# A selective-scan and gated-expert kernel: opening reordered, and one row tile of each batch transposed a phase later

## The reference, cut to what matters

```python
# B=4 batches, L=512 steps, 512 channels, 16 states, 512 model columns
x_in  = in_proj_w @ ctx                       # 512 channels x 512 steps, batch by batch
u     = silu(causal_conv4(x_in) + conv_b)
dt_lo, Bm, Cm = split(x_proj_w @ u)           # 16 + 16 + 16 rows: the small projection
delta = softplus(dt_proj_w @ dt_lo + dt_proj_b)
for t: state = state * exp(delta_t * A) + (delta_t * u_t) * B_t     # per channel, 16 states
       y_t   = sum_n state[n] * C_t[n]
y     = (y + D * u) * silu(layernorm(x))
x2    = x + tanh(g_xattn) * y
h     = layernorm(x2)
sc    = h @ Wr.T; g = softmax(sc) kept at its top 2 and normalised
out   = x2 + tanh(g_ffn) * sum_s g_s (h @ U_s) @ V_s * (0.9 + 0.2 * g @ aw)
```

## Time and profile before

| | us |
|---|---|
| median of 3 runs | 594.83 (594.62 to 600.63) |
| the profiled execution | 593.71 |
| its span in the trace | 592.0 |
| PE busy | 516.1 (87%) |
| POOL busy | 483.2 (82%) |
| DVE busy | 458.4 (77%) |
| ACT busy | 395.5 (67%) |

### The profile page before, as it was taken

How to read it: one execution, slowest core, us unless ns; L and a number is a source line. 1 busy time by engine, 2 the same in 40 slices (tenths; PEclk the granted TensorE clock), 3 DMA queues, 4 the chain that set the end, 5 groups by cost and what they waited for, 6 DMA issues and landing times.

```text
span 592.0 us, 9391 instructions
## 1 busy us (share of the span) xinstructions
PE 516.1 (87%) x3162; PEld 392.7 (66%) x3162; DVE 458.4 (77%) x839; ACT 395.5 (67%) x702; POOL 483.2 (82%) x362
## 2 busy tenths in 40 slices
PE   6658689898985999999969999999699998999686
PEld 2147579767875697769668787677566765676453
DVE  3648799978976999779887999786677878788630
ACT  2366476958773878487946787578579777987321
POOL 0088779979998999979997999699889998888700
PEclk9768899999977999999988999999999999999969
DMA  4198000006520001045220000075000000000000
GB/s 88 40 335 304 2 0 2 37 6 219 172 72 0 2 1 54 0 148 197 90 72 2 19 2 18 6 262 184 19 19 0 19 18 19 19 3 18 19 1 35
DMA packets 17986, 37.29 MB, mean 63 GB/s; under 512 B 5505, under 2 KB 6017, under 8 KB 17938
## 3 DMA queue, kind: packets, MB, share of 16 engines
q1 hardware_dynamic: 17938, 36.69, 17.9%
HBM read 32.23 MB, written 4.46 MB: 62 GB/s over the span
## 4 chain that ended last, share of the span: by engine, by line
PE 52%; POOL 22%; ACT 10%; issue 8%; DVE 5%; DMA 1%; DVEq 0%; POOLq 0%; ACTq 0%; SPq 0%
PE p_s L676 15%; POOL state L504 12%; PE p_y L695 11%; POOL dbu L491 6%; PE p_v L727 5%; PE p_f L718 4%; PE p_tr L644 4%; DVE state L1110 3%; PE p_pr L608 3%; ACT da L895 2%; POOL pair_b L467 2%; PE p_pr L601 1%; PE p_s L601 1%; PE p_pr L619 1%; ACT L847 1%
## 5 line engine op out<-in xcount | busy, mean ns | idle before, releaser
L504 POOL TENSOR_TENSOR state<-state,c_bc 128x1024 f32<-128x1024 f32 (+1 forms) x160 | 307.4, 1929 | 39.4 <-DVE state L1110 36.5
L1110 DVE TENSOR_TENSOR_SCAN state<-da,p_s 128x512 f32<-128x512 f32 (+1 forms) x160 | 175.7, 1105 | 58.3 <-PE p_s L676 54.6
L676 PEld LDWEIGHTS p_s<-pair_b,du_t 128*128 128x128 f32 x1280 | 171.4, 202 | 38.2 <-issue 23.0
L676 PE MATMUL p_s<-pair_b,du_t 128*128 128x128 f32 x1280 | 185.5, 288 | 6.8 <-ACT du_t L853 5.3
L695 PE MATMUL p_y<-ident,state 128*128 128x128 f32 x1024 | 151.7, 277 | 0.5 <-POOL state L504 0.5
L895 ACT ACTIVATE da<-delta,a_neg 128x512 f32<-128x512 f32 (+1 forms) x192 | 120.2, 642 | 25.1 <-DVE state L1110 24.8
L695 PEld LDWEIGHTS p_y<-ident,state 128*128 128x128 f32 x1024 | 121.7, 143 | 20.8 <-issue 18.3
L491 POOL TENSOR_TENSOR dbu<-du,pair_b 128x1024 f32<-128x1024 f32 (+1 forms) x64 | 116.5, 1820 | 0.1
L1110 DVE TENSOR_TENSOR_SCAN state<-p_s,dbu 128x512 f32<-128x512 f32 (+1 forms) x96 | 98.6, 1032 | 1.9 <-POOL dbu L491 1.9
L895 ACT ACTIVATE p_s<-delta,a_neg 128x512 f32<-128x512 f32 (+1 forms) x128 | 73.4, 579 | 38.4 <-DVE state L1110 37.8
L718 PE MATMUL p_f<-u_sb,h_t 128*128 128x512 f32 x112 | 55.2, 595 | 1.5 <-DVE gw L1197 1.5
(11 more groups left out here) (170 smaller groups left out, 624.8 us busy)
## 6 DMA issues: line engine op xcount, KB each, us to landing
c_bc<-bc_rows SPq DMA_DIRECT2D x32, 512.0 KB, 5.9
pair_b<-bc_rows SPq DMA_DIRECT2D x12, 512.0 KB, 5.5
xs<-in_x SPq DMA_DIRECT2D x16, 256.0 KB, 7.4
out<-ot SPq DMA_DIRECT2D x14, 256.0 KB, 2.0
cx<-in_ctx_t SPq DMA_DIRECT2D x4, 512.0 KB, 3.6
u_sb<-in_u_w SPq DMA_DIRECT2D x1, 1024.0 KB, 13.6
v_sb<-in_v_w SPq DMA_DIRECT2D x1, 1024.0 KB, 15.6
out<-state SPq DMA_DIRECT2D x2, 256.0 KB, 2.0
```

The lines of the kernel that those rows point to most:

```text
L504: eng.tensor_tensor(pair, pair, c_bc[:, 2 * p:2 * p + 2, c0:c0 + w], ALU.mult).then_inc(po_cs, 1)
L676: mm = eng.matmul(p_s[g % BANKS][:, t * P:(t + 1) * P], du_t[:, f % 2, t, :], diagonals_of(n // 2)[:, n % 2, c0 // P + t, :], start=(t == ...
L1110: eng.tensor_tensor_scan(slot(g)[:, 0:w], decayed, added, first, ALU.mult, ALU.add).then_inc(ve_scan, 1)
```

## The change

Opening: the small projection takes each block when its u is there, and `in_projection(4)` with its conv moves behind it. x of batches 0 and 1 and the weights U are loaded ahead of the store of B and C instead of among and behind the broadcasts. The z statistics and `scale_of_z(0)` move ahead of phase 0. For states 0 and 1 of phase 0 DVE makes du and dt\*u\*B itself (`first_dbu`), from a broadcast of B's pair 0 that is new; POOL's `times_u(0)` falls away and its diagonals of pair 0 are made after `times_c(0, 0)`. The exponential for A and the two tanh of the gates move ahead of the small projection's copy. From phase 1 on: for T = 0, 4, 8, 12 `normed` moves from n = 15 to n = 0 of the next phase, `turn_h` to its n = 1, `copy_h` from n = 1 to n = 2, and in phases with k = 0 `scale_of_f` stands ahead of `times_c(f, 5)`.

```diff
@@ which tiles have their dt*u*B made where
+    def on_dve(f, n):
+        return f == 0 and n < 2
-    PE_TILES = [(f, n) for f in range(F) for n in range(NS) if not on_pool(f, n)]
+    PE_TILES = [(f, n) for f in range(F) for n in range(NS) if not on_pool(f, n) and not on_dve(f, n)]
-    DIAGONALS = [(b, p) for b in range(B) for p in pe_pairs(b) if not by_act(b, p)]
+    DIAGONALS = [(0, p) for p in pe_pairs(0)[1:] + [0]]
+    DIAGONALS += [(b, p) for b in range(1, B) for p in pe_pairs(b) if not by_act(b, p)]
...
+        def wait_for_du(eng, f):
+            if f:
+                eng.wait_ge(po_du, f)
+            else:
+                eng.wait_ge(ve_du, 1)
@@ SP
+            for k in range(Q):
+                load_x(0, k)
             eng.wait_ge(pe_in, Q)
             load_ctx(1)
-            store_bc(0)
-            broadcast_b(0, 2)
-            broadcast_c(0, 0)
-            broadcast_c(0, 1)
-            broadcast_b(0, 5)
-            for p in range(2, 5):
-                broadcast_c(0, p)
-            for k in range(Q):
-                load_x(0, k)
-            for p in range(5, PAIRS):
-                broadcast_c(0, p)
             for k in range(Q):
                 load_x(1, k)
             eng.dma_start(u_sb[:, :, :], u_w.rearrange("(c p) n -> p c n", p=P)).then_inc(s_uv, 16)
+            store_bc(0)
+            broadcast_b(0, 0)
+            broadcast_c(0, 0)
+            broadcast_b(0, 2)
+            broadcast_c(0, 1)
+            broadcast_c(0, 2)
+            broadcast_b(0, 5)
+            for p in range(3, PAIRS):
+                broadcast_c(0, p)
             eng.dma_start(v_sb[:, :, :], v_w.rearrange("(c p) n -> p c n", p=P)).then_inc(s_uv, 16)
@@ POOL, diagonals, times_u, times_b
+                if (b, p) == (0, 0):
+                    eng.wait_ge(ve_dbu, 2)
...
+                if f == 1:
+                    eng.wait_ge(ve_dbu, 2)
...
+                elif i == 1:
+                    eng.wait_ge(ve_scan, 2)
                 if p == pool_pairs(b)[0]:
-                    eng.wait_ge(po_du, f + 1)
+                    wait_for_du(eng, f)
@@ POOL, order of work
-            diagonals(0, 0)
+            scale_of_z(0)
             diagonals(0, 1)
-            times_u(0)
+            diagonals(0, 2)
             times_b(0, pool_pairs(0)[0])
-            for i in range(2, len(pe_pairs(0))):
+            for i in range(3, len(pe_pairs(0))):
                 diagonals(0, i)
             for f in range(F):
...
                 times_c(f, 0)
+                if f == 0:
+                    diagonals(0, 0)
...
                 if turning:
                     diagonals(b + 1, 0)
+                if k == 0 and STATS.get(f):
+                    scale_of_f(STATS[f][0])
                 times_c(f, 5)
...
-                if STATS.get(f):
+                if k and STATS.get(f):
                     scale_of_f(STATS[f][0])
...
-                if f == 0:
-                    scale_of_z(0)
                 times_c(f, 6)
@@ PE
             def small_projection(b, blocks):
-                eng.wait_ge(ve_u, Q * b + Q)
                 for k in blocks:
+                    eng.wait_ge(ve_u, Q * b + Q if b else k + 1)
...
             def dt_projection(f):
...
                 if f:
                     eng.wait_ge(ve_dl, f)
+                if f > 1:
                     eng.wait_ge(ve_u, min(f + Q, BLOCKS))
...
             eng.wait_ge(s_first, 16)
-            for q in range(5):
+            for q in range(Q):
                 in_projection(q)
             eng.wait_ge(s_second, 16 * 6)
             eng.wait_ge(po_k, 9)
             small_projection(0, range(Q))
             dt_projection(0)
             turn_b(0)
+            in_projection(4)
             turn_du(0)
...
+                    if n == 1 and mid >= 0 and mid % Q == 0:
+                        turn_h(mid)
                     if n == 2:
...
-                    if n == 15 and Q <= f < EARLY + Q:
+                    if n == 15 and Q <= f < EARLY + Q and f % Q:
                         turn_h(f - Q)
@@ ACT
             tanh_v(Q - 1)
-            conv_first(4)
+            eng.wait_ge(s_second, 16 * 6)
+            eng.activation(a_neg[:, :, :], a_neg[:, :, :], ACT.Exp).then_inc(ac_k, 1)
+            eng.wait_ge(s_w, 16 * 5)
+            eng.activation(gx[:, :], gx[:, :], ACT.Tanh).then_inc(ac_k, 1)
+            eng.activation(gf[:, :], gf[:, :], ACT.Tanh).then_inc(ac_k, 1)
...
-            copy_du(0)
...
                     if f == 0 and n == 1:
+                        copy_du(0)
+                        conv_first(4)
+                    if f == 0 and n == 5:
                         tanh_v(4)
...
-                    if n == 1 and mid >= 0:
+                    if n == 0 and mid >= 0 and mid % Q == 0:
+                        normed(mid)
+                    if n == (1 if mid % Q else 2) and mid >= 0:
                         copy_h(mid)
...
-                        if Q <= f < EARLY + Q:
+                        if Q <= f < EARLY + Q and f % Q:
                             normed(f - Q)
@@ DVE
             def scan(f, n):
...
-                if on_pool(f, n):
+                if on_dve(f, n):
+                    eng.wait_ge(ve_dbu, n + 1)
+                    decayed, added = p_s[g % BANKS][:, :], dbu[:, 1, n, :]
+                elif on_pool(f, n):
...
+            def first_dbu(n):
+                if n == 0:
+                    eng.wait_ge(s_bbc[0], 16)
+                eng.tensor_tensor(dbu[:, 1, n, :], du[:, :], rows_of_b(0)[:, n, :], ALU.mult).then_inc(ve_dbu, 1)
...
-            taps(4)
...
+            for q in range(Q):
+                z_statistics(q)
             combine(0)
+            eng.wait_ge(ve_dl, 1)
+            eng.tensor_tensor(du[:, :], delta[:, 0, :], u[:, 0, :], ALU.mult).then_inc(ve_du, 1)
+            eng.wait_ge(ve_du, 1)
+            first_dbu(0)
+            first_dbu(1)
...
                     scan(f, n)
-                    if f == 0 and 8 <= n < 8 + Q:
-                        z_statistics(n - 8)
-                    if f == 0 and n == 4:
+                    if f == 0 and 2 <= n < 5:
+                        tap(4, n - 1)
+                    if f == 0 and n == 6:
                         silu_u(4)
```

More of the change, by code:

```diff
@@ L251, in flamingo @@
         ve_zs = sem("dve_z_statistics")
+        ve_du = sem("dve_du")
+        ve_dbu = sem("dve_dbu")
         ve_scan = sem("dve_scanned")
@@ L328, in broadcasts_of_b @@
         def broadcasts_of_b(b, p):
-            return sum(p in pool_pairs(a) for a in range(b + 1))
+            return sum(p in pool_pairs(a) for a in range(b + 1)) + (p == 0)
         ZOPS = 6
@@ L457, in diagonals @@
                     return
-                if i == 0:
+                if (b, p) == (0, 0):
+                    eng.wait_ge(ve_dbu, 2)
+                if i == 0 or b == 0:
                     eng.wait_ge(ac_turn, TURN["b", b] + 1)
@@ L474, in times_u @@
                 eng.wait_ge(ve_dl, f + 1)
-                if f:
-                    eng.wait_ge(pe_turn, TURN["du", f - 1] + 1)
-                    eng.wait_ge(po_dbu, by_pool[f, pool_pairs(b)[0]])
+                eng.wait_ge(pe_turn, TURN["du", f - 1] + 1)
+                eng.wait_ge(po_dbu, by_pool[f, pool_pairs(b)[0]])
+                if f == 1:
+                    eng.wait_ge(ve_dbu, 2)
                 eng.tensor_tensor(du[:, 0:w], delta[:, f % 2, 0:w], u[:, (Q * b + k) % U_RING, c0:c0 + w],
@@ L665, in make_dbu @@
                 g = NS * f + n
-                if n == 0:
+                if n == 0 or g == 2:
                     eng.wait_ge(ac_turn, TURN["du", f] + 1)
-                if by_act(b, n // 2):
+                if b == 0 and n == 0:
+                    eng.wait_ge(po_diag, DIAGONALS.index((0, 0)) + 1)
+                elif by_act(b, n // 2):
                     if k == 0 and c0 == 0:
@@ L748, in _ @@
                 for n in range(NS):
-                    if not on_pool(f, n):
+                    if (f, n) in by_pe:
                         make_dbu(f, n)
@@ L885, in decay @@
                     eng.wait_ge(ve_dl, f + 1)
-                if on_pool(f, n):
+                if (f, n) not in by_pe:
                     if g >= BANKS:
@@ L979, in _ @@
             copy_b(0)
-            eng.wait_ge(s_second, 16 * 6)
-            eng.activation(a_neg[:, :, :], a_neg[:, :, :], ACT.Exp).then_inc(ac_k, 1)
             softplus(0, 2)
-            copy_du(0)
             eng.wait_ge(ve_k, 4)
@@ L994, in _ @@
                     if f == 0 and n == 1:
+                        copy_du(0)
+                        conv_first(4)
+                    if f == 0 and n == 5:
                         tanh_v(4)
-                    if f == 0 and n == 3:
-                        eng.wait_ge(s_w, 16 * 5)
-                        eng.activation(gx[:, :], gx[:, :], ACT.Tanh).then_inc(ac_k, 1)
-                        eng.activation(gf[:, :], gf[:, :], ACT.Tanh).then_inc(ac_k, 1)
+                    if f == 0 and n == 4:
```

(6 more changed lines are left out.)

## The result

| | before | changed |
|---|---|---|
| median, us | 595.12 (594.62 to 600.63) | 564.53 (564.01 to 565.71) |
| ratio, 95% interval | | 0.947 (0.941 to 0.953) |
| span of the profiled execution | 592.0 | 562.3 |
| first scan | 38.40 | 31.88 |
| opening and phases 0 to 3 | 152.3 | 138.4 |

The median fell by 30.6 us, where 26.3 were forecast. A phase is counted from its first scan to the next phase's. All phases that aren't in the table (7, 10, 11, 14, 15, 18, 19) agree within 0.1 us. So the places are the two that the prediction names: the opening with phases 0 to 3 brings 13.9, the four ends 5.3 + 6.5 + 4.3 + 0.5 = 16.6, and the close behind the last scan takes 0.8 longer: 29.7 in the profiled executions. The other 0.9 of the 30.6 is how the two profiled executions lie to their medians.

The account below looks back on a forecast made before the run. Bounds by phase: POOL and DVE in 2, PE and POOL in 6, PE in 9; POOL for the opening's gain. 11.5 + 4.6 + 5.6 + 3.8 + 0.8 = 26.3 off 593.7 gives 567.4, plus 1.1: 568.5 us; range 560 to 579.

Parts of the forecast that it names:

- Small projection: Opening: last two blocks priced at the slow clock, 3.6 us, ending at 24.5, 2.4 earlier; 4.2 earlier at full clock.
- First scan at 32 to 34: Sign for the opening: scan 0 starts at about 32.8 instead of 38.40 us.
- z's scale before 29: Sign for the opening: `scale_of_z` comes before 29 us, its work lying in POOL's and DVE's idle time.
- POOL bounds: 11.5: Opening and first batch: POOL's chain limits the gain to 11.5 us, between 9 and 14.
- the DVE count: First batch by DVE's work alone: phase 1 at 60.4, phase 2 at 84.4, 14 us earlier than 98.35.
- the 85 to 88: Sign for the first batch: phase 2 begins at 85 to 88 us.
- The ends: Ends of phases 4, 8, 12, 16: moving h removes PE's waits, gaining 4.6, 5.6, 3.8 and 0.8 us.
- the rival that POOL takes it: Ends: only what POOL follows at once is gained, 6.4 instead of 14.8 us, giving 577; chance 0.2.
- One sign: Ends of phases 4, 8, 12: PE waits no more than 1 us for h.
- Only changes place: Ends: POOL's scale merely swaps places with one `times_c` of 2.34 us.
- The clock's return: Phases 9 and 13 back at full clock: 28.5 instead of 31.0 us, and 1.58 us from 20.23 to 18.65.
- The port rule: Opening: DVE instructions with two SBUF inputs and POOL's exclude each other; du could wait 1.09, DVE's 14 becoming 12.9.

Follow-up runs that it names:

- the repetition: The changed kernel run once more with no edit, on another chip beside two later edits: 565.05 us, ratio 0.953.
- the two with filling for PE: Changed kernel with extra identity transpositions in PE's opening waits: 563.77 us; the same plus POOL's broadcast wait filled with diagonals: 566.39 us.
- filled-POOL kernel: Changed kernel with three more POOL diagonals ahead of its first product and B's pair 2 broadcast ahead of C's pair 0: 566.55 us.
- h-only kernel: Kernel before with only the four h moved, including POOL's scale ahead of `times_c(f, 5)`: 580.42 us, ratio 0.974.
- opening-only kernel: Changed kernel with `normed`, `turn_h`, `copy_h` and `scale_of_f` put back in their old places: 585.28 us, ratio 0.982.

## Why the prediction was right, and where its sum was short

**Small projection: both prices are real.** I took the slow one, 3.6, and an end at 24.5. The profiled execution shows 1.93 and an end at 22.8; the same code in the repetition shows 3.45. Of the eight profiled kernels with the small projection block by block and no filling for PE, two show 1.93 and six 3.43 to 3.68; the two with filling for PE show 1.93. Whether TensorE has its higher clock at 20 us differs from one execution to the next. The end comes 1.1 earlier with the fast one, but the first scan only 0.3 (31.9 and 32.2): in the first execution DVE's du and products met POOL's diagonals (0.93 and 2.06), in the second they came after them (0.69 and 1.29). From the projection's end to delta's it was 6.1 us in both, where I had carried over 6.2; delta was there at 28.9 and 30.0, forecast 30.7.

**First scan at 32 to 34:** 31.9, forecast 32.8. In part luck: delta came 1.8 earlier than forecast, and DVE's du and products took 3.0 instead of 2.1. The broadcast was early enough. The first one went out at 25.25 (forecast 26.9), and the first three landed 3.5, 5.4 and 7.6 us after issue, for 3.8 to 8.5 of the first four in the earlier trace rows.

**z's scale before 29:** 27.95. Right, but its worth was hidden in a count of the whole phase. Putting it back made phase 4 start 11.4 us later.

**"POOL bounds: 11.5". This step failed.** POOL's forecast of its first `times_c` of phase 1 (66.3) was nearly met, at 65. But the rule drawn from it, that the batch gains only what POOL gains, was wrong. The phases' starts moved as I had worked out for DVE alone: phase 1 at 60.5 (60.4), phase 2 at 84.5 (84.4, a gain of 13.9), and phase 4 came 13.9 earlier. That the DVE count fits so closely is luck in part: the first scan was 0.9 earlier than in it and phase 0 1.1 longer (28.7, not 27.6). POOL's first `times_c` of phases 1, 2, 3 and 4 came 10.6, 12.1, 12.1 and 13.9 us earlier than before: it lags and catches up. It was idle for 2.1 us in phase 0, nothing in phases 1 and 2, and 1.6 in phase 3, where it was 3.5 before. The filled-POOL kernel confirms that more work done ahead is worth nothing. So phase 2 began at 84.5, outside the 85 to 88 that I had named as a sign.

**The ends.** Forecast 4.6, 5.6, 3.8, 0.8; measured 5.3, 6.5, 4.3, 0.5. Phases 4 + 5 took 56.9 (58.5 forecast), but phase 6 took 29.5 instead of 28.5, with PE and POOL full: a part of the gain is given back one phase later. The larger part stays, so the rival that POOL takes it is false. One sign failed: at the end of phase 4 PE still waits 1.75 us for h, where I had named 1 us as the most and taken nothing in the sum. The rule is the same as in the opening: an engine that is full in one phase follows if it has slack in the next ones. I used it for the ends, and should have used it for the opening.

**The sum.** Against 26.3 forecast, the opening brought 2.4 more (13.9 for 11.5) and the ends 1.8 more (16.6 for 14.8); the close, which I had left out, took 0.8 back. That gives 29.7. The remaining 0.9 of the 30.6 lies between profiled executions and medians.

**"Only changes place", the scale.** It was costed at nothing, yet without it the moved h costs 6.7 us. As the two were changed together the total didn't suffer, but the reason was incomplete: of the 13.4 us that h alone brought, 6.8 are left when the scale stays behind its `times_c`.

**Clock.** The forecast that PE's clock stays full behind phase 4 holds up to 531 us, in the close (where it was at its lower level from 563.6 before). The clock's return was included only for phases 9 and 13, 2.5 + 1.6; filling the stops gave 4.0 by phases, so together these terms had the right size, though 1.2 of it lies in phase 8.

**The port rule.** In the earlier trace rows DVE's 128x64 constant took 1.09 us beside a diagonal; in the changed kernel, with no POOL instruction beside it, it took 0.17. Du and the first product met diagonals too. Timeline of the changed kernel, POOL and DVE:

```profile
28.22 1.10 POOL L483 TENSOR_SCALAR_AFFINE_SELECT pair_b<-b_t 128x1024 f32<-128x1024 f32 x1
28.93 0.93 DVE L1273 TENSOR_TENSOR du<-delta,u 128x512 f32<-128x512 f32 x1
29.27 1.54 POOL L483 TENSOR_SCALAR_AFFINE_SELECT pair_b<-b_t 128x1024 f32<-128x1024 f32 x1
29.90 1.46 DVE L1149 TENSOR_TENSOR dbu<-du,pair_b 128x512 f32<-128x512 f32 x1
```

Du ends at 29.86, 0.54 us behind the first diagonal (28.22 + 1.10 = 29.32); the product ends some 0.54 behind the second (29.27 + 1.54 = 30.81). In the four profiles in which du or a product met a diagonal, all ten of these instructions end 0.54 us behind a diagonal's end, wherever in it they began, and a diagonal that comes behind one takes 1.54 instead of 1.09. So they take turns, and each waits the other out; only some 0.15 us at the start of an instruction (0.69 less 0.54) overlaps. The small DVE constants (128x64 and 128x32, 0.15 to 0.18 us alone) end 0.03 to 0.05 us behind a POOL instruction that they met, in all seventeen cases of the fourteen profiles, and took up to 2.40 us for it. The Trainium skill (SBUF — State Buffer, "Who interferes with whom") speaks of an exclusive lock between the two engines, and the traces agree. What I had worked out from it, one diagonal of 1.09 us, was right too: du and the products took 2.99 us, 1.98 without diagonals. It didn't keep the gain below 13.9, since delta came 1.8 earlier than in the count.

**What stays open.** The medians of the two parts alone (22.0) and together (27.8 to 30.6) differ by 6 to 9 us. The profiled executions differ by 12.4 (4.5 + 12.8 against 29.7), and there the places can be told. The opening with phases 0 to 3 brought 9.8 in the opening-only kernel and 13.9 in the changed one, with the same code in it; the rest of the opening-only kernel, the code of before, took 5.2 longer than before, 3.3 of that in phase 17; and the h-only kernel reached phase 4, over unchanged code, 2.0 later than before. In the opening-only kernel both places have clock stretches at the lower level. Its profiled execution was 3.9 above its median, so these places aren't those of the medians. Why the clock falls in one execution and not in another isn't shown. Nor was each part of the opening taken back by itself: the small projection block by block, `in_projection(4)` behind it and the earlier exponentials were not.

## What to carry to other kernels

When a part is brought forward, don't price it by the fullest engine at that place: look whether that engine has idle time in the next phases, for then, as here, the gain can be what the chain through the others allows. A stop of an engine behind a wait costs more than its length where its clock falls afterwards; check the granted clock of the stretch behind it. And when a wait is moved, follow what releases it: the operation that must come earlier (here POOL's scale, one `times_c` sooner) may decide whether the move is worth anything.

## What the runs showed of the hardware

- The same code has TensorE at its lower or its higher level at one place from execution to execution: four instructions of the small projection took 1.93 us in one and 3.45 in another. The Trainium skill (TensorE: Matmul & The Clock Gate, "What's actually happening") says of a kernel's start that the number of slow matmuls varies from run to run. The traces agree: at the start, four matmuls took over 0.9 us in the changed kernel and six in its repetition, where later ones take 0.59. They show it again in the middle of a kernel: behind a stop of 4.29 us for T = 8, with the same code, the four transpositions of h took 0.66 us in the kernel before and 1.12 in the opening-only kernel.
- Idle waiting can be filled to hold the clock: 24 transpositions of the identity, 2.78 us, in each of three stops made the kernel 4.6 us faster. Where 3.91 us of idle time was left behind them, the clock fell all the same.
- A DVE product of two SBUF inputs (128x512) took 0.69 us alone and 1.46 to 1.57 when it met a diagonal of POOL's, and the diagonal behind it 1.54 instead of 1.09: they take turns by whole instructions. A small `tensor_scalar` of DVE's (128x32), 0.15 us alone, waited out a whole `tensor_tensor` of POOL's and took 2.40.
